# Moving layer-norm statistics and Newton steps between chunks of an attention stage

## The reference

```python
def _layernorm(x, axis=-1, eps=1e-05):
    m = jnp.mean(x, axis=axis, keepdims=True)
    v = jnp.var(x, axis=axis, keepdims=True)
    return (x - m) / jnp.sqrt(v + eps)

# attention: h = 16 heads of 16 features, 4 groups, s = 256
scores = jnp.einsum('bhqd,bhkd->bhqk', q, k) * (1.0 / np.sqrt(d))
scores = jnp.where(causal[None, None, :, :], -jnp.inf, scores)
attn = jax.nn.softmax(scores, axis=-1)
out = jnp.einsum('bhqk,bhkd->bhqd', attn, v)

# feed-forward, with weights made ternary: wu, wg, wd
hidden = jax.nn.silu(up) * gate

x = x + 0.5 * _L0_ffn_ref(_layernorm(x, axis=-1), ...)
x = x + _L0_attn_ref(_layernorm(x, axis=-1), ...)
x = x + 0.5 * _L0_ffn_ref(_layernorm(x, axis=-1), ...)
```

## Time and profile before

| | us |
|---|---|
| median of 3 runs | 585.79 (584.58 to 586.39) |
| profiled execution | 586.84 |
| its span, first to last instruction | 585.10 |
| TensorE matmul busy | 556.2 (95%) |
| VectorE busy | 478.9 (82%) |
| ScalarE busy | 400.1 (68%) |
| GpSimd busy | 169.6 (29%) |

### The profile page before, as it was taken

How to read it: one execution, slowest core, us unless ns; L and a number is a source line. 1 busy time by engine, 2 the same in 40 slices (tenths; PEclk the granted TensorE clock), 3 DMA queues, 4 the chain that set the end, 5 groups by cost and what they waited for, 6 DMA issues and landing times.

```text
span 585.1 us, 12391 instructions
## 1 busy us (share of the span) xinstructions
PE 556.2 (95%) x4244; PEld 344.8 (59%) x4244; DVE 478.9 (82%) x1861; ACT 400.1 (68%) x717; POOL 169.6 (29%) x264
## 2 busy tenths in 40 slices
PE   2989999999999989999999999898999999999998
PEld 2445565655666756666666666563456656566566
DVE  6898978899876889999999998895797688666664
ACT  4857655765745468898888888876666765765642
POOL 3115201101530034554546464666301101100100
PEclk9999999999999999999999999998999999999999
DMA  8711101100104151433323323312201211111112
GB/s 312 224 30 37 18 19 37 36 20 19 38 10 118 34 136 57 92 89 65 103 53 100 85 68 85 81 36 39 38 1 40 69 55 55 36 55 55 36 37 73
DMA packets 72222, 37.90 MB, mean 65 GB/s; under 512 B 35520, under 2 KB 71616, under 8 KB 72128
## 3 DMA queue, kind: packets, MB, share of 16 engines
q1 hardware_dynamic: 72160, 37.11, 24.6%
HBM read 18.22 MB, written 10.49 MB: 49 GB/s over the span
## 4 chain that ended last, share of the span: by engine, by line
PE 76%; DVE 16%; ACT 2%; issue 2%; POOL 2%; DMA 1%; SPq 1%; DVEq 0%; ACTq 0%; POOLq 0%
PE bank L1169 33%; PE bank L1181 17%; DVE sm_out L986 6%; PE bank L1268 5%; PE bank L1325 5%; PE bank L1295 5%; PE bank L1336 4%; PE bank L1350 2%; PE bank L1341 2%; PE bank L1145 1%; DVE hid L855 1%; DVE stats L735 1%; POOL xn L413 1%; ACT shared L596 1%; DVE hl L870 1%
## 5 line engine op out<-in xcount | busy, mean ns | idle before, releaser
L486 ACT ACTIVATE silu<-bank,w_scale 128x512 f32<-128x512 f32 x128 | 87.4, 683 | 112.9 <-PE bank L1169 112.9
L986 DVE CUSTOM_DVE_ANT_0 sm_out<-bank,mask 128x256 f16<-128x256 f32 (+1 forms) x512 | 151.1, 352 | 12.7 <-PE bank L1295 12.0
L855 DVE SCALAR_TENSOR_TENSOR hid<-silu,h_unit,bank 128x512 f32<-128x512 f32 x128 | 94.9, 742 | 63.9 <-ACT silu L486 63.5
L1181 PE MATMUL bank<-wT_down,hh 128*128 128x256 f16 x512 | 118.2, 273 | 2.5 <-DVE hl L870 2.3
L1181 PE MATMUL bank<-wT_down,hl 128*128 128x256 f16 x512 | 118.2, 273 | 0.0
L1169 PE MATMUL bank<-xh,wT_up 128*128 128x512 f16 x256 | 98.0, 383 | 1.1 <-DVE xl L799 0.7
L870 DVE TENSOR_TENSOR hl<-hid,hh 128x512 f16<-128x512 f32 x128 | 98.5, 769 | 0.0
L1169 PE MATMUL bank<-xh,wT_gate 128*128 128x512 f16 x256 | 97.5, 381 | 0.9 <-DVE hid L855 0.9
L1169 PE MATMUL bank<-xl,wT_up 128*128 128x512 f16 x256 | 98.0, 383 | 0.0
L1169 PE MATMUL bank<-xl,wT_gate 128*128 128x512 f16 x256 | 97.3, 380 | 0.0
L422 POOL TENSOR_TENSOR xnl<-xn,xnh 128x1024 f16<-128x1024 f32 x13 | 28.3, 2176 | 213.0 <-ACT xn L525 177.8
(11 more groups left out here) (134 smaller groups left out, 798.2 us busy)
## 6 DMA issues: line engine op xcount, KB each, us to landing
q_st<-q_scratch SPq DMA_DIRECT2D x32, 256.0 KB
q_scratch<-q_hl SPq DMA_DIRECT2D x16, 256.0 KB, 2.3
out_dram<-x SPq DMA_DIRECT2D x7, 512.0 KB, 3.0
x<-in_x_dram SPq DMA_DIRECT2D x1, 3072.0 KB, 15.6
k_scratch<-k_hl SPq DMA_DIRECT2D x16, 128.0 KB, 2.4
k_st<-k_scratch SPq DMA_DIRECT2D x16, 128.0 KB
x<-in_x_dram SPq DMA_DIRECT2D x2, 512.0 KB, 4.6
shared<-in_w_up_t_dram SPq DMA_DIRECT2D x2, 512.0 KB, 6.1
```

Source lines behind the costliest of these rows:

```text
L486: act.activation(silu[:, e % 2, :], U[e % 2][:, :], ACT.Silu, scale=w_scale[:, 0:1]).then_inc(silu_ready, 1)
L855: dve.scalar_tensor_tensor(out=hid[:, e % 4, :], in0=silu[:, e % 2, :], scalar=h_unit[:, 0:1], in1=GT[e % 2][:, :], op0=ALU.mult, op1=ALU. ...
L986: ins = dve.tensor_tensor_reduce(sm_out[:, i, cols], SM[i][:, cols], mask[:, S - size:S], -1.0 / MAX_UNIT, -MASKED, ALU.add, ALU.min, rowm ...
L1181: ins = pe.matmul(ACC[t % 2][:, 0:D], part[:, par, e, t * P:(t + 1) * P], wT_down[:, e, :], start=(e == 0 and part is hh), stop=(e == NE - ...
```

## The change

The statistics that chunk 0 takes for a later chunk move from its even sequence to its odd one, to the same groups 1 and 2 of it. The Newton steps of batch 7 move from chunk 0 to the same groups of chunk 1. And in all three chunks with Newton steps the last four steps and the shift stand in group 2 of the odd sequence, no longer in group 1. Nothing is added or removed; TensorE, ScalarE, GpSimd and SyncE issue the same instructions in the same order.

```diff
--- before.py
+++ after.py
@@ -1036,17 +1036,17 @@
                 for k in range(4):
                     b, odd = 2 * c0 + k, k % 2
                     c = c0 + k // 2
-                    batch = {0: 7, 2: 8, 4: 9}.get(c, 0)
+                    batch = {1: 7, 2: 8, 4: 9}.get(c, 0)
                     for g in range(G):
                         lead = (4 * b + g + 6, (k + (g + 6) // 4) % 2, (g + 2) % 4)
                         ahead = not (last and (k == 3 or (k == 2 and g >= 2)))
 
                         steps = {(0, 3): range(0, 4), (1, 0): range(4, 8),
-                                 (1, 1): range(8, 12)}.get((odd, g), ()) if batch else ()
+                                 (1, 2): range(8, 12)}.get((odd, g), ()) if batch else ()
                         for i in range(3):
                             if ahead and not (not odd and g == 0 and i == 0):
                                 row_max(*lead, i, batch, steps)
-                            if not odd and c < 5:
+                            if odd == (c == 0) and c < 5:
 
                                 q = NC + 6 + c
                                 if g == 1 and i == 0:
```

## The result

| | before | after |
|---|---|---|
| median of 20 runs, us | 585.76 | 586.82 |
| range of the runs, us | 584.58 to 586.92 | 586.08 to 588.71 |
| profiled execution, us | 586.84 | 586.69 |
| its span, us | 585.10 | 584.9 |

The medians differ by 1.1 us. The ratio, taken over the runs' means, is 1.0023, with a 95% interval of 1.0016 to 1.0031, which is 1.3 us: slower, beyond the scatter, but by less than the 0.3% that the prediction took as the least that counts as a difference. The forecast was 587.2, with a range of 585.7 to 588.8 and "within 0.3%" as the likeliest.

What follows compares the result with a forecast made beforehand. TensorE was taken to set the pace in attention, VectorE where Newton steps lie. -0.20 + 0.49 + 0.83 + 0.30 = +1.42 us on the median 585.79 gave 587.2 us, range 585.7 to 588.8.

Steps and rivals of the forecast that it cites:

- Part 1: Chunk 0's even half and odd start: falls to TensorE's 9.60 us plus a DMA loss of 0.15 that stays, -0.20.
- Part 2: Chunk 0's odd sequence: gains all statistics, loses four Newton steps and the shift, VectorE sets the pace, +0.49 us.
- Part 3: Chunk 1: gains twelve Newton steps on top of its statistics and becomes like chunk 2, +0.83 us.
- Part 4: Last four steps one group later in chunks 1, 2, 4: TensorE's wait moves, GpSimd blocking adds +0.1 us each.
- rival 1: Odd third group, chunks 1, 2, 4: two steps blocked by GpSimd, +0.76 us a chunk, 589.2 us; chance 0.15.
- rival 2: Odd sequence hides statistics like the even one, chunk 0 gives back 0.83, chunk 1 takes it: 0, 585.8 us; chance 0.20.
- rival 3: TensorE keeps its 0.57 us gain in each of three chunks: -1.86 in all, 583.9 us; chance 0.10.

Runs made afterwards that it cites:

- e3: Before, with only batch 7's Newton steps moved from chunk 0 to chunk 1, all statistics staying in even sequences; 585.76 us.
- e8: Before, with the statistics of chunks 1 and 3 moved to their odd sequences; 587.82 us, ratio 1.0034.
- e1: Changed kernel, with the last four Newton steps back in group 1 of the odd sequence; 586.53 us, ratio 1.0010 against before.
- e2: Before, with only the last four Newton steps and the shift moved to group 2 of the odd sequence; 585.64 us.
- e9: Changed kernel, with steps 8 to 11 and the shift of batches 7, 8, 9 reading one operand from PSUM; 585.85 us.
- e4: Before, with Newton steps in chunks 1, 3, 5: even groups 1 and 3, the last four and shift in odd group 3; 584.98 us.
- e5: e4 with the last four Newton steps and the shift in group 1 of the odd sequence; 583.83 us, ratio 0.9964 against before.
- e6: e5 with Newton steps 4 to 7 in group 0 of the odd sequence; 584.79 us, ratio 0.9993 against before.
- e10: e5 with steps 8 to 11 and the shift of batch 9 in group 1 of chunk 6's even sequence; 583.73 us.
- e7: Changed kernel, with steps 9 to 11 of batches 7, 8, 9 reading one operand from PSUM; 586.27 us, ratio 1.0004 against before.

## Why the prediction was right, step by step

**Part 1, even half of chunk 0: -0.20 forecast, -0.36 measured.** The step that was off is that "it stays", of the 0.15 that chunk 0 loses to the maxima's DMA. It is no property of chunk 0's list: TensorE's wait there was 0.4 us before and 0.2 after, 0.8 in e3, and identical lists spread over 0.36 us. My lower bound, -0.35, was this case.

The reason for the 0.15 was wrong as well. In chunk 2 the steps at 280.80 and 282.32 take 0.56 and 0.15; the same two steps in chunk 0 take 0.15 (227.07) and 0.64:

```profile
228.25 0.64 DVE L771 SCALAR_TENSOR_TENSOR rstd<-newton,rstd 128x8 f32<-128x8 f32 x1
```

```profile
228.24 0.64 POOL L368 TENSOR_SCALAR_AFFINE_SELECT hl<-hl 128x512 f32<-128x512 f32 x1 [0.48 <-ACT hl L596]
```

GpSimd's masks ran later there against VectorE's list: the first began at 227.12, just behind one step, the second at 228.24, just ahead of the other. In e8, with the same list in chunk 0, the first mask began at 226.95, the two steps took 0.56 and 0.15, and the chunk lasted 19.61 like chunk 2. So the 0.15 was a longer wait of Newton steps for GpSimd in that execution, and it left chunk 0 with the steps; whether the late maxima set it off is not shown. The three statistics before 217.96 lengthened the wait from 1.05 to 2.04, as worked out (2.07).

**Part 2, odd sequence of chunk 0: +0.49 forecast, +0.44 measured.** 10.25 instead of 10.30. e8 repeats the figure in two other chunks. The reason given, that VectorE's list is longer than TensorE's pace there, holds: it is busy 10.16 of 10.25.

**Part 3, chunk 1: +0.83 forecast; +0.83 in e1 and e3**, where it stands apart from part 4.

**Part 4: +0.1 a chunk forecast, +0.09 measured** in chunks 1, 2 and 4 (changed kernel against e1, e2 against before). The wait of TensorE moved one group on (0.80 to 0.74), as laid out; in its old place nothing was left of it, where I had put about 0.2, and late in chunk 0 it waited 0.35 and 0.50, where I had put over 1. Of the blocked steps I had the second and the last, at 0.07 and 0.16 over their price; they show 0.09 and 0.14 (0.25 and 0.30 against 0.16). The shift, to which I gave perhaps 0.1, took 0.17, its usual length. e9 shows that these are waits for GpSimd: 0.25 us a chunk goes when none of the moved steps has two SBUF operands. The port lock that the Trainium skill describes ("SBUF — State Buffer", its section on SBUF's two separate sides) agrees with both halves of this, the waiting and its absence; that the GpSimd operation has to read SBUF was not varied here.

**The sum: +1.42 forecast, +1.17 in the chunks, +1.1 timed.** Of the 0.25 too much, 0.16 is part 1, 0.05 part 2 and 0.03 part 4. Nothing gave it back, as said, but for 0.2 of waits for transferred maxima in chunk 6, which differ between executions anyway.

**The rivals.** Blocking that decides (rival 1) needed two full blocks in the group with the moved steps; e2 and the changed kernel show +0.09 a chunk there instead of +0.76. That it could have been otherwise is shown by e4, whose group of 4.20 has two such steps, and it was close here: the third moved step begins at 288.31, just before one mask ends (287.77 + 0.63 = 288.40) and 0.16 before the next begins (288.47). Rival 1's condition, steps that fall just behind the start of a mask, was not met by that much. Give and take (rival 2) is refuted by e3 against e1 and by e8. TensorE's lead (rival 3) is refuted by e2.

**What was luck.** The forecast did not know that executions of one kernel differ by some 1.2 us for a reason outside it. It put the sum on a median of three runs of before, 585.79, which lies between the two kinds; the 20 runs then had a median of 585.76. With three runs of one kind it could have stood 0.3 us lower or 0.9 higher. The terms themselves did not need this luck, because they came from stretches of chunks and not from spans.

## What to carry to other kernels

Where two engines run in step, work moved on the one with the longer list costs what its target stretch lacks in waits: here statistics of 1.65 us were free ahead of a wait of TensorE's making and cost 1.06 us in an odd sequence whose waits come to some 0.5, and a step taken from a full group and put into the next full one only moves the other engine's wait. So add up, per stretch between two waits, what the engine has to do and what its partner allows, and put small work only where the difference is positive; e5 did this and won 1.8 us where the tried change lost 1.1. The sum is not enough by itself: e4 and e6 looked nearly as good by it, and their steps met GpSimd's masks and cost 0.84 a chunk. Small instructions that read SBUF are to be laid beside GpSimd's timeline, since here some lasted four times their length there. And a stretch that is to price moved work must hold the whole of it.

## What the runs showed of the hardware

In all profiled executions with a mean clock of 0.997 TensorE's granted clock dips once, late in the attention stage, in before to a mean of 0.83 over 10 us (the page's slice shows 0.8). Ahead of the dip, which began there between 402 and 403 us, the engine had waited 0.81 and 0.64 us for other engines, but in the changed kernel's profile, without a dip, it had waited 0.81 and 0.64 at the same places. The dip costs 0.9 to 1.3 us by the medians of before and after. What decides it is open. It is as large as the effect that was to be measured, and the share of such executions differs (9 of 20 for the changed kernel, 24 of 35 in one series of before), so medians of few runs can move by an us without any cause in the kernel.

The wait of a VectorE instruction for GpSimd ends with the GpSimd operation, stands inside the length that the profile shows for the instruction, and makes up to 0.49 us for a step of 0.15 (0.64 at 228.25 before). With one of two operands in PSUM the same kind of instruction at the same place takes 0.16. Steps that read one tensor from SBUF (L758, L764) waited the same way in e4, e5, e6 and e10, 0.57 to 0.64 us long; statistics instructions did not. Over the traces of before, after and all experiments but e7, 135 steps with no operand in PSUM begin inside a mask or a residual add and at least 0.16 before its end: 134 of them end 0 to 0.03 us behind it, and the one exception begins at the very time of the mask (227.10 in e2). The twelve such steps with an operand in PSUM, all in e9, end before it.
